# GpSimd clips every fourth probability block of the first cross-attention, with eight places for the blocks and later value products

## The chip, the cores and the metric

The kernel runs on one core of one Trainium2 chip. The metric is device time in microseconds, the median of several runs. The core's engines are TensorE (PE in the profile; PEld is its weight load), VectorE (DVE), ScalarE (ACT), GpSimd (POOL) and SyncE (SP, which here only starts transfers). Each engine works through its own list of instructions in order and waits on semaphores for the others.

## The reference

Two decoder layers on x of 2 x 512 x 256, with a context of 2 x 1024 x 192. Each layer has self-attention, cross-attention and a feed-forward part, with a layer norm behind each:

```python
x = _layernorm(x + _L0_attn_ref(x, ...))          # A0: 16 heads, causal
x = _layernorm(x + _L0_xattn_ref(x, ctx, ...))    # X0: 16 heads over 1024 keys
x = _layernorm(x + _L0_ffn_ref(x, ...))
x = _layernorm(x + _L1_attn_ref(x, ...))          # A1
x = _layernorm(x + _L1_xattn_ref(x, ctx, ...))    # X1
x = _layernorm(x + _L1_ffn_ref(x, ...))           # 8 experts, 2 chosen
```

The change is in X0:

```python
attn = jnp.einsum('bhqd,bhkd->bhqk', q, k) * scale
attn = jnp.clip(attn, -CLAMP, CLAMP)
attn = jax.nn.softmax(attn, axis=-1)
attn = jnp.where(jnp.any(jnp.isnan(attn)), 1.0 / Nkv, attn)
x = jnp.einsum('bhqk,bhkd->bqhd', attn, v).reshape(B, Nq, Cq)
return x @ Wo + bo
```

## The kernel before

A function builds one list of steps for the whole program (`build_schedule`), and each engine's block walks that list and emits the steps that are its own. So the list alone sets each engine's order. The first layer's attentions, A0 and X0, come from `paired_stream`. Their 16 heads are worked in groups of four, per batch: eight groups for A0, then eight for X0 (`PAIRS`).

X0 handles each group twice. The first pass makes scores with queries on the partitions, 16 items per group (S1, L1574, in rounded fp32), and VectorE reduces each to row maxima (M1, L1312, "halves", two rows of 512 keys at a time, negated). MN (L1318, L1319) joins and clamps them, and a TensorE transposition (unit "mt") brings them to the layout in which VectorE adds them to the queries (UD of "mt"). The second pass makes scores with keys on the partitions, 16 items per group: eight blocks j of 128 keys, each in two halves pr of two heads (S2, L1596). ScalarE takes the exponential straight into `prob_a` and sums it for the check on NaNs (E2, L1130). VectorE clips each item of 128 x 1024 to between exp(-60) and exp(60) (CL, L1326). The value product of a block takes both halves (PV, L1619) and adds into `p_out`; the last one of a group is followed by ScalarE's copy of `p_out` (DN, L1146), a transposition ("dt"), and VectorE's scaling into `normed`. While one group is in its second pass, the next is in its first.

One step n of the list holds, in this order: what empties the unit of the step before (UA, UD and the cast KF on GpSimd for the key and query operands), S2 and E2 of one item, S1 and M1 of one item of a later group, the clip of the item of the step before, at most one PV, and one unit (key, query or value product, transposition). A block's product is put into the list once its second half's clip is two steps old (`age(...) >= 2`); blocks go in order (`adds`), at most one per step. So in the steady state there is a product in every second step.

Both kinds of score block use the same ring of three places in PSUM, `p_ring` (`RING`). By the ring's order, S2 of step n waits for the maximum (M1) of step n - 2, and S1 of step n for the exponential (E2) of step n - 1 (`slot_free`). `prob_a` in SBUF has `NPT` = 6 places: E2 waits for the product of the block of six items ago. The first product of a group waits for the copy of `p_out` of the group before.

GpSimd has little to do: in A0 it clears the later keys (TM, L1042), in X0 it casts the key and query operands (KF, L1033, three per group), adds the biases (BA, L1075) and inverts deviations of the layer norms (LP, L1081, L1082). It scales a1_wq (L1050) and x1_wq (L1054) later.

The lines that matter for the order and the waits:

```python
        if adds and age("CL" if adds[0][0] == "X0" else "TM", *adds[0], 1) >= 2:
            c = adds.pop(0)
            sched.add("PV", *c)
```

```python
                    wait(act, "S2", *key)
                    if n >= NPT:
                        wait(act, "PV", *prob_list[n - NPT][:4])
```

## Time and profile before

| | |
|---|---|
| runs before | 1327.78, 1327.05, 1320.21 us; median 1327.05 |
| the profiled execution | 1310.7 us, span 1309.0 us |
| busy share of the span | TensorE 89%, VectorE 56%, ScalarE 43%, GpSimd 7% |
| mean granted clock of TensorE | 0.952 |
| X0's exponentials | 202.8 to 465.5 us of the span |
| clips of X0 on VectorE (L1326) | 128, 89.5 us, 700 ns each on average |
| maxima of X0 (L1312, 128x1024) | 128, 155.6 us, 1219 ns each |

A row of the timeline has the start in us from the span's start, the duration, the engine and line, the operation, what it writes and reads, the shapes, and in brackets how long the engine was idle before and who ended that. Times in the rows are microseconds, where ns isn't written. Instructions of one engine can overlap by about 0.1 us at their ends. The ends of matmuls are modelled, so what waits for them tells more than their durations.

### The profile page before, as it was taken

Reading aid. Unit: us, or ns where it says so; the run is one execution under the profiler, and the core shown is the slowest. Engines: PE = TensorE matmul, PEld = TensorE weight load, DVE = VectorE, ACT = ScalarE, POOL = GpSimd, SP = SyncE. Lnnn points to the kernel's source line nnn. Section 1 sums busy time; section 2 is a strip of 40 time slices with the busy share of each in tenths; the row PEclk is TensorE's granted clock in tenths of the full one; section 3 lists DMA queues with packets and bytes.
Section 4 is the critical chain, followed back from the end, with each engine's and each line's share of the span. In section 5 each row is a group of like instructions: output and inputs, shape, how many; then the busy total and the mean of one; then the engine's idle time right before and its main releaser. Section 6 shows DMA issues by size and latency. Waiting matters only on the chain.

```text
span 1309.0 us, 20311 instructions
## 1 busy us (share of the span) xinstructions
PE 1163.7 (89%) x7602; PEld 737.1 (56%) x7602; DVE 734.4 (56%) x1083; ACT 560.2 (43%) x1078; POOL 86.6 (7%) x126
## 2 busy tenths in 40 slices
PE   4998988898998864897799999999999999998886
PEld 2454443232322233786477777767777777776545
DVE  3447567888889747344265645654445554654322
ACT  1444424555555632120266654555334553453230
POOL 0112301000000002000000000000000000000120
PEclk8899778999999977999899999999999999999989
DMA  6011002000000020000533222323533333210000
GB/s 178 11 50 26 1 1 57 1 1 1 1 1 1 1 81 1 1 1 1 139 74 74 66 66 46 80 57 89 116 92 82 81 82 81 47 36 1 1 17 16
DMA packets 46819, 57.44 MB, mean 44 GB/s; under 512 B 12539, under 2 KB 25350, under 8 KB 46726
## 3 DMA queue, kind: packets, MB, share of 16 engines
q1 hardware_dynamic: 42966, 52.48, 16.4%
q10 hardware_dynamic: 3760, 3.67, 0.9%
q8 instruction: 64, 1.05, 0.3%
q14 instruction: 29, 0.24, 0.1%
HBM read 15.23 MB, written 3.15 MB: 14 GB/s over the span
## 4 chain that ended last, share of the span: by engine, by line
PE 77%; DVE 10%; issue 6%; ACT 3%; POOL 1%; DMA 1%; SPq 1%; POOLq 0%; ACTq 0%; DVEq 0%
PE p_unit L1529 20%; PE p_ring L1529 11%; PE p_ring L1630 9%; PE p_out L1653 8%; PE p_ring L1549 8%; PE p_ring L1596 7%; PE p_out L1619 6%; PE p_ring L1574 2%; PE p_unit L1715 2%; PE p_unit L1673 1%; DVE probT_b L1342 1%; PE p_ring L1588 1%; DVE stats L1245 1%; ACT prob_a L1130 1%; POOL m_z L1059 1%
## 5 line engine op out<-in xcount | busy, mean ns | idle before, releaser
L1148 ACT ACTIVATE probT_b<-p_ring 128x512 f32<-128x512 f32 x144 | 84.5, 598 | 260.0 <-PE p_ring L1630 259.6
L1312 DVE TENSOR_REDUCE halves<-p_ring 128x2 f32<-128x1024 f32 x128 | 155.6, 1219 | 44.2 <-PE p_ring L1574 44.0
L1342 DVE COPY probT_b<-p_ring 128x512 f32<-128x512 f32 x112 | 77.4, 691 | 173.7 <-PE p_ring L1630 173.7
L1294 DVE TENSOR_REDUCE nmax<-p_ring 128x2 f32<-128x1024 f32 (+1 forms) x128 | 155.9, 1218 | 23.3 <-PE p_ring L1549 23.3
L1130 ACT ACTIVATE prob_a<-p_ring 128x1024 f32<-128x1024 f32 x128 | 130.5, 1023 | 89.5 <-PE p_ring L1596 89.2
L1116 ACT ACTIVATE prob_b<-p_ring,nmax 128x512 f32<-128x512 f32 (+1 forms) x192 | 158.7, 835 | 2.9 <-DVE nmax L1294 2.6
L1549 PE MATMUL p_ring<-stacks 128*128 128x512 f32 x512 | 150.8, 416 | 4.5 <-ACT prob_b L1116 4.5
L1630 PE MATMUL p_ring<-ident,prob_b 128*128 128x128 f32 x1024 | 134.6, 274 | 0.0
L1630 PEld LDWEIGHTS p_ring<-ident,prob_b 128*128 128x128 f32 x1024 | 115.8, 141 | 27.7 <-issue 25.8
L1596 PE MATMUL p_ring<-x_q,x_kq 32*128 32x512 f32 x512 | 117.8, 646 | 0.2
L1549 PEld LDWEIGHTS p_ring<-stacks 128*128 128x128 f32 x512 | 87.0, 190 | 17.1 <-ACT prob_b L1116 5.1
L1326 DVE TENSOR_SCALAR prob_a<-prob_a 128x1024 f32<-128x1024 f32 x128 | 89.5, 700 | 8.2 <-ACT prob_a L1130 8.2
L1312 DVE TENSOR_REDUCE wide_max<-p_ring 128x2 f32<-128x256 f32 (+3 forms) x64 | 52.4, 823 | 63.7 <-PE p_ring L1567 63.7
L1574 PE MATMUL p_ring<-x_kqF 32*128 32x512 f32 x256 | 66.2, 515 | 23.4 <-ACT prob_a L1130 23.0
L1596 PEld LDWEIGHTS p_ring<-x_q,x_kq 32*128 32x128 f32 x512 | 37.5, 186 | 63.8 <-issue 45.4
L1619 PE MATMUL p_out<-prob_a,x_v 128*32 128x512 f32 x512 | 68.2, 604 | 2.7 <-issue 1.8
L1653 PE MATMUL p_out<-probT_b,a_v 128*64 128x128 f32 x1024 | 70.0, 279 | 0.0
L1653 PE MATMUL p_out<-probT_b,x_v 128*64 128x128 f32 x1024 | 69.6, 279 | 0.0
L1653 PEld LDWEIGHTS p_out<-probT_b,a_v 128*64 128x64 f32 x1024 | 54.6, 136 | 23.4 <-issue 17.5
L1653 PEld LDWEIGHTS p_out<-probT_b,x_v 128*64 128x64 f32 x1024 | 54.6, 136 | 21.9 <-issue 11.3
L1529 PE MATMUL p_unit<-ctxT,x_wk 128*128 128x512 f32 x128 | 65.2, 633 | 0.3
L1485 DVE TENSOR_TENSOR splitL_b<-p_unit,splitH_b 128x512 fp32r<-128x512 f32 x44 | 30.4, 691 | 60.8 <-ACT splitH_b L1199 54.7
(199 smaller groups left out, 1610.4 us busy)
## 6 DMA issues: line engine op xcount, KB each, us to landing
stacks<-splitH_b SPq DMA_DIRECT2D x144, 128.0 KB, 2.3
stacks<-splitL_b SPq DMA_DIRECT2D x144, 128.0 KB, 2.4
a_st<-a_image SPq DMA_DIRECT2D x64, 32.0 KB, 1.8
ctx_raw<-in_ctx ACTq DMA_DIRECT2D x1, 1536.0 KB, 15.2
x<-in_x ACTq DMA_DIRECT2D x2, 512.0 KB, 5.5
k_words<-in_L_ffn_k SPq DMA_DIRECT2D x1, 1024.0 KB, 6.7
a_wq<-in_L_attn_Wq SPq DMA_DIRECT2D x1, 1024.0 KB, 6.0
a_wo<-in_L_attn_Wpost SPq DMA_DIRECT2D x1, 1024.0 KB, 8.6
```

The source lines that it names most:

```text
L1116: ins = nc.scalar.activation(prob_b[:, n % NP_SLOTS, a * 512:a * 512 + w_all], p_scores[:, n % 2, a * 512:a * 512 + w_all], ACT.Exp, bias= ...
L1130: nc.scalar.activation(prob_place(key), slot_of("S2", key), ACT.Exp, accum_out=x0_sums[:, m:m + 1]).then_inc(done["E2"], 1)
L1294: nc.vector.tensor_reduce(nmax[:, n % 4, 0:heads], src, AX.X, ALU.max, negate=True).then_inc(done["M"], 1)
L1312: nc.vector.tensor_reduce(to, src, AX.X, ALU.max, negate=True).then_inc(done["M1"], 1)
L1342: keep_turned(dve, key, lambda o, i: nc.vector.tensor_copy(o, i)).then_inc(done["VD"], 1)
L1529: ins = nc.tensor.matmul(o, a, m, start=(n == 0), stop=(n == len(pairs) - 1))
L1549: ins = nc.tensor.matmul(p_scores[:, n % 2, 512 * a:512 * a + 512], st[:, q_at:q_at + 128], st[:, k_at:k_at + 512], start=(part == 0), sto ...
L1574: ins = nc.tensor.matmul(o[:, aa, :], x0_kqF[r:r + 32, place, 2, 128 * i:128 * i + 128], x0_kqF[r:r + 32, place, hf, :], start=True, stop= ...
L1596: ins = nc.tensor.matmul(o[:, aa, :], x0_kq[r:r + 32, place, j // 4, 128 * (j % 4):128 * (j % 4) + 128], x0_q2[r:r + 32, G % 2, :], start= ...
L1619: ins = nc.tensor.matmul(p_out[32 * a:32 * a + 32, lo:T], v, prob_place((*key, a // 2))[:, a % 2, at:at + T - lo], start=(c == 0), stop=end)
L1630: ins = nc.tensor.transpose(p_turn[:, half, 128 * j:128 * j + 128], prob_b[:, n % NP_SLOTS, 128 * bl:128 * bl + 128], ident[:, :])
L1653: ins = nc.tensor.matmul(p_out[rows * a:rows * a + rows, 128 * i:128 * i + 128], values(L, b, h, j), probT[:, n % places, 4 * in_tile + j ...
```

## The change

GpSimd gets a new kind of step, CP, for the second half (pr = 1) of every odd block j of X0: four of each group's 16 items, 32 of 128. It runs the same `tensor_scalar` (max, then min) on the same place of `prob_a`. The product of such a block is put into the list once its clip is four steps old instead of two; since blocks go in order, the even block behind it is late too. `prob_a` has eight places instead of six. The new function `clipped_by` says whose clip a product waits for.

```diff
--- before.py
+++ after.py
@@ -52,7 +52,7 @@
 NP_SLOTS = 3
 RING = 3
 HELD = 3
-NPT = 6
+NPT = 8
 UNDER = 60.0
 LOW, HIGH = float(np.exp(-UNDER)), float(np.exp(UNDER))
 NC1 = 7
@@ -110,6 +110,11 @@
 def prob_items(grp):
 
     return [(*grp, j, pr) for j in range(NKV // 128 if grp[0] == "X0" else 3) for pr in range(2)]
+
+
+def clipped_by(it):
+
+    return "TM" if it[0] == "A0" else "CP" if it[3] % 2 == 1 and it[4] == 1 else "CL"
 
 
 def blocks_at(j):
@@ -193,7 +198,7 @@
                     sched.add("MN", *it[:3])
                 owed.insert(0, ("mt", *it[:3]))
         for it in clean:
-            sched.add("CL" if it[0] == "X0" else "TM", *it)
+            sched.add(clipped_by(it), *it)
             if it[4] == 1:
                 adds.append(it[:4])
         clean = fresh
@@ -203,7 +208,7 @@
             owed.append(("dt", *grp))
             if grp[2] % 2:
                 owed.append(("rb", *grp[:2], grp[2] // 2))
-        if adds and age("CL" if adds[0][0] == "X0" else "TM", *adds[0], 1) >= 2:
+        if adds and age(clipped_by((*adds[0], 1)), *adds[0], 1) >= (4 if clipped_by((*adds[0], 1)) == "CP" else 2):
             c = adds.pop(0)
             sched.add("PV", *c)
             if c[3] == prob_items(c[:3])[-1][3]:
@@ -693,7 +698,7 @@
             "UA": "unit_emptied_by_act", "UD": "unit_emptied_by_dve", 
             "BA": "bias_added", "LS": "variances_ready", "LP": "deviations_inverted",
             "LN": "x_normalised", "XA": "x_rounded", "XD": "x_rest_ready", "FW": "signs_ready",
-            "FS": "hidden_split", "CL": "probs_clipped", "DN": "outputs_kept", "NF": "nans_counted", "GN": "nans_replaced",
+            "FS": "hidden_split", "CL": "probs_clipped", "CP": "probs_clipped_by_pool", "DN": "outputs_kept", "NF": "nans_counted", "GN": "nans_replaced",
             "ZD": "gates_by_dve", "ZA": "gates_by_act", "ZP": "roots_ready",
         }
         done = {k: sem(v) for k, v in names.items()}
@@ -1031,6 +1036,10 @@
                     if 4 * b + g >= HELD:
                         wait(pool, "S1", *max_items(PAIRS[8 + 4 * b + g - HELD])[-1])
                     nc.gpsimd.tensor_copy(x0_kqF[:, place, part, :], x0_kq[:, place, part, :]).then_inc(done["KF"], 1)
+                elif kind == "CP":
+                    wait(pool, "E2", *key)
+                    t = prob_place(key)
+                    nc.gpsimd.tensor_scalar(t, t, LOW, HIGH, ALU.max, ALU.min).then_inc(done["CP"], 1)
                 elif kind == "TM":
                     j = key[3]
                     wait(pool, "E2", *key)
@@ -1602,7 +1611,7 @@
                     L, b, g, j = key
                     grp = key[:3]
                     for pr in range(2):
-                        wait(pe, "CL" if L == "X0" else "TM", *key, pr)
+                        wait(pe, clipped_by((*key, pr)), *key, pr)
                     if j == 0:
                         back = pair_back(grp, 1)
                         if back:
```

The list changes TensorE's order. Here is TensorE's list in a stretch of X0 from one query product ("xT,x_wq") to the copy's transposition ("ident,raw") and the first products of the next group. `x_q,x_kq` is S2, `x_kqF` S1, `prob_a,x_v` the value product. Before:

```order
L1529 MATMUL p_unit<-xT,x_wq 128x512 x2
L1596 MATMUL p_ring<-x_q,x_kq 128x512 x2
L1574 MATMUL p_ring<-x_kqF 128x512 x2
L1619 MATMUL p_out<-prob_a,x_v 32x512 x4
L1596 MATMUL p_ring<-x_q,x_kq 128x512 x2
L1574 MATMUL p_ring<-x_kqF 128x512 x2
L1596 MATMUL p_ring<-x_q,x_kq 128x512 x2
L1574 MATMUL p_ring<-x_kqF 128x512 x2
L1619 MATMUL p_out<-prob_a,x_v 32x512 x4
L1685 MATMUL p_unit<-ident,raw 128x128 x4
```

The same stretch of the change, from the same query product (its lines are numbered nine higher):

```order
L1538 MATMUL p_unit<-xT,x_wq 128x512 x2
L1605 MATMUL p_ring<-x_q,x_kq 128x512 x2
L1583 MATMUL p_ring<-x_kqF 128x512 x2
L1605 MATMUL p_ring<-x_q,x_kq 128x512 x2
L1583 MATMUL p_ring<-x_kqF 128x512 x2
L1605 MATMUL p_ring<-x_q,x_kq 128x512 x2
L1583 MATMUL p_ring<-x_kqF 128x512 x2
L1628 MATMUL p_out<-prob_a,x_v 32x512 x4
L1605 MATMUL p_ring<-x_q,x_kq 128x512 x2
L1583 MATMUL p_ring<-x_kqF 128x512 x2
L1628 MATMUL p_out<-prob_a,x_v 32x512 x4
```

Before, the last product of a group (the first of the two above) and the first product of the next stand two steps apart, with the copy of `p_out` in the step between; now they stand in neighbouring steps, and everywhere in X0 the products stand in pairs, with two steps without one behind them.

VectorE's list in the same stage, before (`TENSOR_SCALAR prob_a` is the clip, `TENSOR_REDUCE` the maximum):

```order
L1312 TENSOR_REDUCE halves<-p_ring 128x2
L1326 TENSOR_SCALAR prob_a<-prob_a 128x1024
L1312 TENSOR_REDUCE halves<-p_ring 128x2
L1326 TENSOR_SCALAR prob_a<-prob_a 128x1024
L1312 TENSOR_REDUCE halves<-p_ring 128x2
L1326 TENSOR_SCALAR prob_a<-prob_a 128x1024
L1312 TENSOR_REDUCE halves<-p_ring 128x2
L1326 TENSOR_SCALAR prob_a<-prob_a 128x1024
```

And of the change:

```order
L1335 TENSOR_SCALAR prob_a<-prob_a 128x1024
L1321 TENSOR_REDUCE halves<-p_ring 128x2
L1335 TENSOR_SCALAR prob_a<-prob_a 128x1024
L1321 TENSOR_REDUCE halves<-p_ring 128x2
L1335 TENSOR_SCALAR prob_a<-prob_a 128x1024
L1321 TENSOR_REDUCE halves<-p_ring 128x2 x2
L1335 TENSOR_SCALAR prob_a<-prob_a 128x1024
```

One clip in four is gone, so two maxima follow each other there; the clip stands on GpSimd, between its casts:

```order
L1042 TENSOR_SCALAR prob_a<-prob_a 128x1024 x3
L1038 CAST x_kqF<-x_kq 128x512
L1042 TENSOR_SCALAR prob_a<-prob_a 128x1024
L1038 CAST x_kqF<-x_kq 128x512 x2
L1042 TENSOR_SCALAR prob_a<-prob_a 128x1024 x3
```

GpSimd's list had only the casts between the bias addition and the layer norm behind X0.

## Rows read from the trace of the kernel before

**Rows 1.** Busy time of each engine in two head groups of X0 (columns: span, busy times with counts, clock, DMA).
```profile
275.27:310.63 35.36, 32.28 (x188) 10.90 (x190) 29.99 (x37) 20.26 (x37) 1.85 (x4) 1.00 0.00 1
...
414.91:445.61 30.70, 27.31 (x176) 8.72 (x178) 27.51 (x36) 18.16 (x34) 0.00 (x0) 1.00 0.00 1
```

**Rows 2.** The chain that ended last from 245 to 387 us, its shares by line.
```profile
by line: PE p_ring L1596 33.8%; PE p_out L1619 22.7%; PE p_unit L1529 16.8%; issue 12.6%; PE p_ring L1574 7.0%; ACT prob_a L1130 2.9%; PE p_unit L1685 1.7%; PE p_unit L1693 1.7%; PE p_unit L1715 0.8%; ACTq L719 0.3%
```

**Rows 3.** Waits in the group 275.27 to 310.63 us (total us, times, longest us).
```profile
ACT prob_a L1130 <- PE p_ring L1596: 11.7, 11, 2.0
PEld p_ring L1574 <- ACT prob_a L1130: 7.1, 6, 1.6
...
DVE halves L1312 <- PE p_ring L1574: 5.3, 8, 2.1
```

**Rows 4.** Timeline of ScalarE in the clean stretch (start, duration, line, operation).
```profile
296.35 1.02 ACT L1130 ACTIVATE prob_a<-p_ring 128x1024 f32<-128x1024 f32 x1 [1.64 <-PE p_ring L1596]
297.27 0.20 ACT L1130 ACTIVATION_READ_ACCUMULATOR prob_a<-p_ring 128x1 f32 x1
...
300.12 1.02 ACT L1130 ACTIVATE prob_a<-p_ring 128x1024 f32<-128x1024 f32 x1 [1.65 <-PE p_ring L1596]
```

**Rows 5.** Timeline of TensorE's matmuls, same stretch.
```profile
297.52 0.50 PE L1574 MATMUL p_ring<-x_kqF 32*128 32x512 f32 x2 [0.75 <-ACT prob_a L1130]
297.95 1.06 PE L1619 MATMUL p_out<-prob_a,x_v 128*32 128x512 f32 x8
298.95 0.70 PE L1596 MATMUL p_ring<-x_q,x_kq 32*128 32x512 f32 x2
...
299.41 1.13 PE L1596 MATMUL p_ring<-x_q,x_kq 32*128 32x512 f32 x6
```

**Rows 6.** Timeline of VectorE, same stretch.
```profile
297.54 0.68 DVE L1326 TENSOR_SCALAR prob_a<-prob_a 128x1024 f32<-128x1024 f32 x1
298.14 1.22 DVE L1312 TENSOR_REDUCE halves<-p_ring 128x2 f32<-128x1024 f32 x1
299.27 0.68 DVE L1326 TENSOR_SCALAR prob_a<-prob_a 128x1024 f32<-128x1024 f32 x1
300.17 1.22 DVE L1312 TENSOR_REDUCE halves<-p_ring 128x2 f32<-128x1024 f32 x1 [0.21 <-PE p_ring L1574]
```

**Rows 7.** Groups of GpSimd's instructions by shape (busy us, mean ns of one).
```profile
L1042 POOL TENSOR_SCALAR_AFFINE_SELECT prob_a<-prob_a 128x256 f32<-128x256 f32 x32 | 13.0, 410 | 50.3 <-ACT prob_a L1134 50.3
...
L1042 POOL TENSOR_SCALAR_AFFINE_SELECT prob_a<-prob_a 128x512 f32<-128x512 f32 x16 | 10.2, 641 | 24.2 <-ACT prob_a L1134 24.2
...
L1050 POOL TENSOR_SCALAR a_wq<-a_wq 128x2048 f32<-128x2048 f32 x1 | 5.5, 5464 | 6.9 <-DMA a_wo<-in_L_attn_Wpost 6.9
...
L1054 POOL TENSOR_SCALAR x_wq<-x_wq 128x1024 f32<-128x1024 f32 x1 | 2.8, 2795 | 34.8 <-DMA x_bo<-in_L_xattn_bout 34.8
```

**Rows 8.** Timeline of GpSimd, the bias addition of the second batch.
```profile
212.36 2.34 POOL L1075 TENSOR_TENSOR x<-x,x_bo 128x1024 f32<-128x1024 f32 x1 [11.36 <-PE p_unit L1673]
```

**Rows 9.** Timeline of VectorE beside it: the clip.
```profile
212.46 2.79 DVE L1326 TENSOR_SCALAR prob_a<-prob_a 128x1024 f32<-128x1024 f32 x1
```

**Rows 10.** Timeline of all engines, the bias addition of the first batch.
```profile
137.04 2.36 POOL L1075 TENSOR_TENSOR x<-x,x_bo 128x1024 f32<-128x1024 f32 x1
...
138.05 1.23 DVE L1312 TENSOR_REDUCE wide_max<-p_ring 128x2 f32<-128x1024 f32 x1 [0.71 <-PE p_ring L1567]
```

**Rows 11.** ScalarE's copy of p_out, by its line (ns: min/median/max).
```profile
L1146 ACT ACTIVATE raw<-p_out x16: 590/592/603, 77.2 to 479.0; 128x512 f32<-128x512 f32 x16
```

**Rows 12.** End of X0: ScalarE's last sum, then VectorE's NaN count and replacement.
```profile
465.34 0.19 ACT L1130 ACTIVATION_READ_ACCUMULATOR prob_a<-p_ring 128x1 f32 x1
...
465.56 0.29 DVE L1330 TENSOR_TENSOR x_sums<-x_sums 128x128 f32<-128x128 f32 x1 [0.37 <-ACT prob_a L1130]
...
467.39 1.29 DVE L1338 COPY_PREDICATED outT_n<-x_nan,x_mean 128x1024 f32<-128x1024 int32 x1
```

**Rows 13.** The chain in order of time: a key product.
```profile
307.61 1.91 PE p_unit L1529 x4
```

## The prediction

> **What bounds the kernel now.** I first took the stage: the change touches the clips of X0, the first cross-attention, and the step at which its value products are issued. By the groups of rows for one head group, a group of sixteen steps lasts 35.36 us, TensorE has work for 32.28, VectorE for 29.99 and ScalarE for 20.26, at the full clock of 1.00 (2.4 GHz) [rows 1]. There are seven such intervals between the eight head groups, most of this length; the last, where the maxima run out, has 30.70 us [rows 1]. The chain of this stage is made of TensorE's products, 12.6% of issue and 2.9% of exponentials; no VectorE line is among the names of this stretch [rows 2]. The waits name the loop: ScalarE waits 11.7 us per group for score blocks (L1596), and TensorE waits for ScalarE's exponential to empty a place of the ring (7.1 us), while VectorE waits 5.3 us for maximum blocks [rows 3].
>
> The timeline shows the loop, which takes two steps. An exponential starts at 296.35, its sum is read by 297.47, the maximum block that takes its place in the ring starts at 297.52 [rows 4, 5]. The value product starts at 297.95 (0.43 later) and the next score block at 298.95 (1.00 later). The next exponential starts at 300.12, 1.17 later [rows 5, 4]. Sum: 1.12 + 0.05 + 0.43 + 1.00 + 1.17 = 3.77 us for two steps, 7.53 for four. VectorE is not in this loop but runs close beside it: a maximum occupies it 1.13 us (298.14 to 299.27), a clip 0.60 (297.54 to 298.14), so four of each need 6.92 of 7.53 us; its one idle gap per two steps is 0.21 us [rows 6]. The second maximum ends at 299.36, and a score block follows at once at 299.41 [rows 6, 5]. So VectorE has about 0.6 us to spare in four steps, and what delays it by more delays everything.
>
> **The change, part by part.**
>
> *32 of 128 clips leave VectorE.* VectorE saves 0.60 us of its order for each: 2.4 us per group, 0.6 in each four steps. By itself that is worth nothing, since the loop above has no clip in it.
>
> *GpSimd clips instead.* The trace has no such clip. The nearest row is the scaling of x1_wq, the same shape with one operation instead of two: 2.80 us; double the width took 5.46, so it is linear [rows 7]. From below, the triangle clearing of 256 and 512 elements took 0.41 and 0.64 us, which makes 1.10 us for 1024; from above I take 5.46, as if each operation were a pass of its own. I take 2.80, since that row is the same instruction. GpSimd's own time is covered: the loop of four steps is 7.5 us, its only other work here are three short casts per group, and the value product now waits four steps behind the clip. With 5.46 us it is covered only just.
>
> *What GpSimd's clip does to VectorE.* This is the term that decides. One row of the trace has a VectorE clip beside a long GpSimd operation: the bias addition ran from 212.36 to 214.70, and the clip that started at 212.46 took 2.79 us instead of 0.68: it ended 0.55 us behind GpSimd's end [rows 8, 9]. It did not run slower, it stood still. A maximum beside the same addition (137.04 to 139.40) took its usual 1.23 us [rows 10]. So I take it that a clip on VectorE waits until GpSimd's instruction has ended, and a maximum does not. The Trainium skill (SBUF — State Buffer, "Who interferes with whom") says this too: a tensor_scalar in a two-port mode and a GpSimd instruction exclude each other for the whole instruction, and a tensor_reduce never contends; the trace agrees, 2.79 us against 0.68.
>
> Between two maxima VectorE nearly always has a clip due. If GpSimd's clip starts as a maximum starts, 1.13 us of it lie under the maximum and the next clip waits 2.80 - 1.13 = 1.67 us. If it starts right in front of a VectorE clip, that one waits 2.80. The exponential of such a block ends at 297.47 and VectorE's next clip starts at 297.54 [rows 4, 6], so at first it is the long case; once VectorE lags, it is the short one. Four steps then cost VectorE 4 x 1.13 + 3 x 0.60 + 1.67 to 2.80 = 8.0 to 9.1 us, against 7.53: VectorE becomes the bound, and late maxima hold the ring's places, so that score blocks and exponentials are late next. Over a group: four waits of 2.25 (the middle) are 9.0 us, minus 2.4 saved, is 6.6 us more in VectorE's order. Its idle time there is 5.3 us [rows 3]; much of it lies behind the three key and query products, where it can be used only if a wait falls there. I estimate that half to two thirds are used, 3.3 us. That leaves +3.3 us per group, and +23 us over seven intervals. Bounds: with all 5.3 used and short waits 4 x 1.67 - 2.4 - 5.3 = -1.0, no loss; with none used and long waits 11.2 - 2.4 = +8.8 per group, +62.
>
> *Value products later and in pairs.* An odd block's product now waits four steps, and the even one behind it in the list follows a step later. The order rows show pairs in neighbouring steps, then two steps without one. Two things follow. In the clean stretch the loop gets shorter where VectorE allows it: with the same pieces, the two exponentials beside the value products are hidden and the walk of four steps comes to 6.85 us instead of 7.53. Against that, the first value product of a head group now stands one step behind the last of the group before, and both use p_out: it must wait for ScalarE to copy p_out (DN). ScalarE does that behind the exponential of the step between. TensorE then waits from the score block on for 1.17 + 1.02 + 0.59 = 2.8 us instead of 0.98 [rows 4, 5, 11], +1.8 us once per group. Before, a whole step without a product lay between. Two of the dearer steps (a value product and a key or query product of 1.91 us [rows 13]) now stand side by side as well, which I estimate at +0.6 per group; the net without any blocking (two clean stretches of four steps per group) is 8 x 1.8 + 7 x 0.6 - 14 x 0.68 = +9 us. With VectorE as the bound neither the gain nor most of the loss shows, since both waits run at the same time. I take 0 here; the bounds are -10 and +15.
>
> *Eight places instead of six.* An exponential waits for the product of eight blocks ago. TensorE's order puts that product at least two steps ahead, so there is no wait, as there was none before. Without the two places the later products would stop ScalarE.
>
> *The end of the stage.* The last clip is GpSimd's. The last exponential's sum is read at 465.53, and GpSimd runs from 465.6 to 468.4. VectorE's NaN count starts at the same time, and reads twice from SBUF [rows 12]. If it is blocked as well, replacing the NaNs (467.39) and the projection behind it come up to 2.8 us later; if not, the last value product comes about 1 us later. I take +2.
>
> Sum: 23 + 0 + 2 = +25 us. The profiled execution took 1310.7 us (span 1309.0), so its counterpart is 1336. The three timed runs lie higher, 1320.2 to 1327.8 with a median of 1327.05, so the predicted median is 1352.
>
> **The rivals.**
>
> *GpSimd's two-operation clip is much longer than 2.80.* For it: the row that I use has one operation, and GpSimd is slow at that shape already. At 3.5 us each wait is 0.7 longer, 28 x 0.7 = +20: 1372. At 5.46 four steps cost 6.32 + 4.33 = 10.65 us instead of 7.53, 28 x 3.1 = +87: about 1414. Against it: the rows for 1024 and 2048 show a rate set per element, which a second operation on the same element need not change.
>
> *The clip is short or doesn't block.* Then only the order counts, +9: 1336, no measurable change. For it: GpSimd's clearing of the same tile runs at a pace of 1.10 us per 1024, and such a clip would hide under one maximum. Against it: 2.80 for the nearest instruction, and rows 8 and 9. The Trainium skill (GPSIMD Engine Reference, "Engine selection") calls GpSimd about as fast as the line for one input; by that rule the clip would take about 1 us and the time be this rival's. The 2.80 us row speaks against it.
>
> *Faster.* If the blocking is absent or falls mostly into the product stretches, and the pairs save their 0.68 us in every four steps, 28 x 0.68 = -19: 1308. It decides once 20 of the 28 cycles gain and the wait for the p_out copy hides behind the ring's own wait. Against it: that copy stands behind an exponential in ScalarE's order, every time.
>
> **How the numbers follow.** Blocking at about 2.80 us (median 1352, own range 1335 to 1365): 0.60. A longer clip: 0.20. Short or unblocked: 0.14. Faster: 0.06. The range 1334 to 1386 takes in the first case, longer clips up to about 4 us, and the upper half of the third; it leaves out the rest, some 0.2. One per cent is 13 us, about what a measurement of this kernel can tell from no change. Slower by more than that (over 1340): 0.53 + 0.20 + 0.02 = 0.75. Faster (under 1314): 0.06. Within: 0.19.
>
> **What would show it.** Right: GpSimd rows of the clip near 2.8 us, 32 of them; VectorE clips in the same stage with a median of 0.68 but some thirty of 2 us or more, each ending about 0.55 us behind a GpSimd clip; VectorE's waits for maximum blocks down from 5.3 to 2 us or less per group; a group of about 38.5 instead of 35.36 us; VectorE clips and maxima in the chain of this stage. The step on the products is right if TensorE waits at the first value product of each group for ScalarE's copy of p_out. Wrong: VectorE clips that stay at 0.68 beside GpSimd's, or GpSimd clips of 4 us and more. Stages before 200 us and behind 470 us should differ by no more than the shift.

## The result, and the profile after

The changed kernel took 1351.18 us in the median of four runs (1340.28 to 1373.43). The kernel before took 1323.63 us in four (1319.42 to 1327.78), and the ratio is 1.0214, with an interval of 1.0161 to 1.0266: slower by 2.1%. A median here is of all executions of a kernel, while a ratio with its interval leaves out those over 1.5% above the kernel's fastest (one of four here, and one of 1944.64 us in pool_two below), so it is not the quotient of the medians. The forecast time of 1352 is met. The mechanism that I gave most of it to is not what happened.

The page of the profiled execution after, first the span, the busy times and the granted clock of TensorE in 40 slices, then from the groups VectorE's maxima (L1321), GpSimd's clips (L1042) and VectorE's clips (L1335):

```profile
span 1351.5 us, 20309 instructions
...
PE 1196.3 (89%) x7602; PEld 749.6 (55%) x7602; DVE 718.0 (53%) x1051; ACT 561.0 (42%) x1078; POOL 202.9 (15%) x158
...
PEclk8995866879999986799899999999999999999998
...
L1321 DVE TENSOR_REDUCE halves<-p_ring 128x2 f32<-128x1024 f32 x128 | 155.0, 1219 | 75.8 <-PE p_ring L1583 74.6
...
L1042 POOL TENSOR_SCALAR prob_a<-prob_a 128x1024 f32<-128x1024 f32 x32 | 117.1, 3658 | 107.5 <-ACT prob_a L1139 107.5
...
L1335 DVE TENSOR_SCALAR prob_a<-prob_a 128x1024 f32<-128x1024 f32 x96 | 72.0, 750 | 14.3 <-ACT prob_a L1139 14.3
```

A GpSimd clip is longer than I took it for (3.66 us in the mean, forecast 2.80). VectorE's clips are hardly longer than before: 750 ns in the mean, 683 in the median. TensorE has the same 7602 matmuls, yet 1196.3 us of busy time, where the kernel before had 1163.7. Its mean granted clock was 0.923, before 0.952.

The head groups of X0, each from its first exponential of the second pass to the next group's (the columns as in [rows 1]):

```profile
218.67:259.89 41.22, 34.59 (x164) 12.81 (x168) 31.07 (x37) 19.10 (x36) 14.15 (x5) 0.71 0.08 21
259.89:302.22 42.33, 36.70 (x184) 11.41 (x185) 28.05 (x33) 19.75 (x36) 16.77 (x8) 0.84 0.00 1
302.22:341.38 39.16, 33.41 (x188) 11.05 (x190) 28.15 (x33) 20.46 (x37) 16.23 (x8) 0.96 0.00 1
341.38:377.95 36.57, 31.52 (x184) 10.46 (x186) 27.97 (x33) 19.76 (x36) 16.23 (x8) 1.00 0.00 1
377.95:415.54 37.59, 31.84 (x188) 10.83 (x190) 28.15 (x33) 20.47 (x38) 16.24 (x8) 1.00 0.00 1
```

Before, the same seven intervals lasted 37.1, 35.4, 35.4, 35.4, 35.4, 33.6 and 30.7 us, all but the first at the clock of 1.00 ([rows 1] has the third and the seventh). The first one before:

```profile
202.79:239.90 37.11, 31.51 (x172) 11.29 (x176) 32.16 (x40) 19.12 (x35) 2.74 (x2) 0.91 0.05 10
```

After, the seven sum to 262.5 us against 242.8. Three of them ran at a lower clock and carry 14.9 of the 19.7 us; the four at 1.00 are longer by 1.2, 2.2, 0.9 and 0.5. The last part, up to the last exponential, has 25.0 us against 18.8. So X0 is 26 us longer, and what lies behind it is not (845 us in both). The 15.9 us by which X0 starts later in this execution lie ahead of every clip and product that the change moves; only the eight places reach that far back, since A0 uses them too. In a second execution of the same kernel (below) they are 2.3. In order_only, with the same order and places, X0 starts 3.9 us earlier than before, and in places, with the eight places alone, 17.1 later. This part varies from trace to trace by more than its own size, and I don't count it to the change.

The waits of the group 377.95 to 415.54 (total us, times, longest), to be held against [rows 3], and the chain from 341.4 to 481 us, against [rows 2]:

```profile
ACT prob_a L1139 <- PE p_ring L1605: 12.0, 14, 2.4
...
DVE halves L1321 <- PE p_ring L1583: 9.2, 6, 2.7
...
PE p_out L1628 <- issue: 1.9, 1, 1.9
```

```profile
by line: PE p_ring L1605 27.5%; PE p_out L1628 18.0%; issue 12.6%; DVE halves L1321 11.1%; PE p_unit L1538 11.0%; PE p_ring L1583 6.4%; DVE prob_a L1335 5.1%; DVE wide_max L1328 2.0%; PE p_unit L1702 1.8%; ACT prob_a L1139 1.4%; PE p_unit L
```

I had forecast that VectorE's wait for maximum blocks falls from 5.3 to 2 us or less. It rose to 9.2: over a group VectorE has more time to spare than before. It is on the path in places, though: its maxima and clips, which weren't among the names of [rows 2], are 16% of the chain now. New among the waits is their last line: a wait of TensorE's at a value product, once in the group. Here it stands, TensorE first, then ScalarE (start, duration, ..., idle time before it in brackets):

```profile
389.49 0.70 PE L1605 MATMUL p_ring<-x_q,x_kq 32*128 32x512 f32 x2
389.63 0.50 PE L1583 MATMUL p_ring<-x_kqF 32*128 32x512 f32 x2
390.02 0.59 PE L1605 MATMUL p_ring<-x_q,x_kq 32*128 32x512 f32 x2
392.47 1.07 PE L1628 MATMUL p_out<-prob_a,x_v 128*32 128x512 f32 x8 [1.85 <-issue]
```

```profile
390.66 1.02 ACT L1139 ACTIVATE prob_a<-p_ring 128x1024 f32<-128x1024 f32 x1 [1.09 <-PE p_ring L1605]
391.58 0.19 ACT L1139 ACTIVATION_READ_ACCUMULATOR prob_a<-p_ring 128x1 f32 x1
391.68 0.59 ACT L1155 ACTIVATE raw<-p_out 128x512 f32<-128x512 f32 x1
```

The group's first value product starts at 392.47, 0.2 us behind the end of ScalarE's copy of `p_out`, which stands behind an exponential; TensorE did nothing for 1.85 us. The profile names "issue" as the releaser, which says only that it shows no event for it; the copy's end is what fits. This line's group, summed over the program, has 13.0 us of such idle time, seven times 1.85. Before it had 1.8, a single wait of the same kind at the first product of the last group (450.80). After, then before:

```profile
L1628 PE MATMUL p_out<-prob_a,x_v 128*32 128x512 f32 x512 | 74.5, 656 | 13.1 <-issue 13.0
```

```profile
L1619 PE MATMUL p_out<-prob_a,x_v 128*32 128x512 f32 x512 | 68.2, 604 | 2.7 <-issue 1.8
```

So six of the seven are new, 11.2 us. That is the wait that I priced right, +1.8 us per group, and then counted as 0.

### The profile page after: what moved, and what is told of

Read it like the earlier page. It is cut to its first block, busy times and chain, and to the rows that moved or that the text cites. A ratio compares the mean times of both kernels' runs of the same rounds, so it can differ in the third digit from the quotient of the medians.

```text
span 1351.5 us, 20309 instructions
## 1 busy us (share of the span) xinstructions
PE 1196.3 (89%) x7602; PEld 749.6 (55%) x7602; DVE 718.0 (53%) x1051; ACT 561.0 (42%) x1078; POOL 202.9 (15%) x158
## 4 chain that ended last, share of the span: by engine, by line
PE 77%; DVE 11%; issue 6%; ACT 3%; DMA 1%; POOL 1%; SPq 1%; POOLq 0%; DVEq 0%; ACTq 0%
PE p_unit L1538 20%; PE p_ring L1538 11%; PE p_ring L1639 9%; PE p_out L1662 8%; PE p_ring L1558 8%; PE p_ring L1605 6%; PE p_out L1628 6%; DVE halves L1321 2%; PE p_ring L1583 2%; PE p_unit L1724 2%; PE p_unit L1682 1%; PE p_ring L1597 1%; DVE prob_a L1335 1%; DVE probT_b L1351 1%; PE p_ring L1576 1%
## 5 line engine op out<-in xcount | busy, mean ns | idle before, releaser
L1321 DVE TENSOR_REDUCE halves<-p_ring 128x2 f32<-128x1024 f32 x128 | 155.0, 1219 | 75.8 <-PE p_ring L1583 74.6
L1042 POOL TENSOR_SCALAR prob_a<-prob_a 128x1024 f32<-128x1024 f32 x32 | 117.1, 3658 | 107.5 <-ACT prob_a L1139 107.5
L1605 PE MATMUL p_ring<-x_q,x_kq 32*128 32x512 f32 x512 | 130.2, 684 | 0.0
L1090 POOL TENSOR_SCALAR veps<-mv 128x4 f32<-128x4 f32 x12 | 3.4, 281 | 722.1 <-DVE mv L1376 722.1
L1321 DVE TENSOR_REDUCE wide_max<-p_ring 128x2 f32<-128x256 f32 (+3 forms) x64 | 52.6, 824 | 75.5 <-PE p_ring L1576 75.4
L1583 PE MATMUL p_ring<-x_kqF 32*128 32x512 f32 x256 | 69.3, 546 | 19.3 <-ACT prob_a L1139 19.0
L1628 PE MATMUL p_out<-prob_a,x_v 128*32 128x512 f32 x512 | 74.5, 656 | 13.1 <-issue 13.0
L1335 DVE TENSOR_SCALAR prob_a<-prob_a 128x1024 f32<-128x1024 f32 x96 | 72.0, 750 | 14.3 <-ACT prob_a L1139 14.3
L1605 PEld LDWEIGHTS p_ring<-x_q,x_kq 32*128 32x128 f32 x512 | 40.9, 200 | 60.7 <-issue 27.1
L1662 PEld LDWEIGHTS p_out<-probT_b,x_v 128*64 128x64 f32 x1024 | 54.6, 136 | 21.9 <-issue 11.3
```

What stands on the lines that cost most here:

```text
L1042: nc.gpsimd.tensor_scalar(t, t, LOW, HIGH, ALU.max, ALU.min).then_inc(done["CP"], 1)
L1321: nc.vector.tensor_reduce(to, src, AX.X, ALU.max, negate=True).then_inc(done["M1"], 1)
L1583: ins = nc.tensor.matmul(o[:, aa, :], x0_kqF[r:r + 32, place, 2, 128 * i:128 * i + 128], x0_kqF[r:r + 32, place, hf, :], start=True, stop= ...
L1605: ins = nc.tensor.matmul(o[:, aa, :], x0_kq[r:r + 32, place, j // 4, 128 * (j % 4):128 * (j % 4) + 128], x0_q2[r:r + 32, G % 2, :], start= ...
L1628: ins = nc.tensor.matmul(p_out[32 * a:32 * a + 32, lo:T], v, prob_place((*key, a // 2))[:, a % 2, at:at + T - lo], start=(c == 0), stop=end)
L1662: ins = nc.tensor.matmul(p_out[rows * a:rows * a + rows, 128 * i:128 * i + 128], values(L, b, h, j), probT[:, n % places, 4 * in_tile + j ...
```

## The experiments

Two theories stood against each other. *Blocking*: GpSimd's clip holds VectorE's up. *Order*: the new places of the value products, above all of the first of a group behind the copy of `p_out`, cost the time, whoever clips.

### after_again: the changed kernel once more

> The changed kernel once more, to see how much of its profiled +42.6 us (1353.3 against 1310.7) is the granted clock. In its trace only four of eight head groups ran at the full clock of 1.00, and those are 0.5 to 2.2 us longer than before, +4.8 us together; the other four at clocks of 0.71 to 0.96 are 4 to 7 us longer, and the part ahead of the first second-pass item was 15.9 us longer at a lower clock too. If the clock is chance, the ratio of this kernel to the one before comes to 1.01 or less and the group times at full clock repeat. If a lower clock comes with the change, the ratio stays near 1.02 and the mean clock under 0.94.

1357.23 us against 1316.76, ratio 1.0255 (1.0177 to 1.0334). X0 lasts 288.9 us (287.6 in the first profile), with the intervals 42.4, 42.3, 37.6, 36.6, 39.2, 34.5, 31.2 and the clocks 0.72, 0.84, 1.00, 1.00, 0.96, 1.00, 1.00. The loss and its shape repeat; which group has the lower clock changes.

### order_only: the changed order, all clips on VectorE

```diff
-                elif kind == "CL":
+                elif kind in ("CL", "CP"):
...
-                    nc.vector.tensor_scalar(pr, pr, LOW, HIGH, ALU.max, ALU.min).then_inc(done["CL"], 1)
+                    nc.vector.tensor_scalar(pr, pr, LOW, HIGH, ALU.max, ALU.min).then_inc(done[kind], 1)
```

> The changed order of value products and the eight places, but all 128 clips on VectorE (in the changed kernel's order). If GpSimd's clip is what costs (by blocking VectorE's), this kernel is near the kernel before: a group at full clock at most 36 us, total within +9 us. If the order of the products costs, a full-clock group takes 36.6 and 37.6 us in turn as in the changed kernel, and the total is the changed kernel's within 0.5%, or a little more since VectorE has its four clips back.

1368.49 us, ratio 1.0299 (1.0228 to 1.037). With no clip on GpSimd the whole loss is there, so blocking is not needed for it. Its fifth interval, and of TensorE's timeline one first product of a group:

```profile
363.02:407.03 44.01, 39.84 (x188) 12.11 (x189) 30.00 (x37) 20.40 (x37) 1.84 (x4) 0.81 0.00 1
```

```profile
294.58 1.06 PE L1624 MATMUL p_out<-prob_a,x_v 128*32 128x512 f32 x8 [1.85 <-issue]
```

The same 1.85 us, and no group at the full clock. Behind the first interval, the recorded stretches at the lower level (1.2 GHz) begin at 255.2, 296.1, 337.1, 378.0, 422.4, 456.5 and 487.3 us, and the seven standstills end at 254.2, 294.6, 335.5, 377.5, 421.6, 456.5 and 486.1: each of them has such a stretch behind it, by at most 1.6 us.

### even: GpSimd's clips, but every product of X0 four steps late

With one delay for all blocks, a product stands in every second step again, and two steps lie between the groups, as before the change.

```diff
-        if adds and age(clipped_by((*adds[0], 1)), *adds[0], 1) >= (4 if clipped_by((*adds[0], 1)) == "CP" else 2):
+        if adds and age(clipped_by((*adds[0], 1)), *adds[0], 1) >= (4 if adds[0][0] == "X0" else 2):
```

> GpSimd keeps its 32 clips, but every block's product waits four steps behind its clip, so that products stand in every second step again, as before the change. If the pairs and the neighbouring first product cost the time, a full-clock group is back at 35.4 us and the total is within 0.5% of the kernel before. If GpSimd's clip costs by itself, the group stays at 36.5 us or more and the total at +10 us or more.

1328.41 us, ratio 1.0071 (1.004 to 1.0102): over two thirds of the loss are gone with all 32 clips still on GpSimd. Its windows:

```profile
207.70:249.15 41.45, 34.85 (x164) 12.42 (x168) 31.22 (x37) 19.12 (x36) 14.68 (x5) 0.71 0.08 21
249.15:284.50 35.35, 31.55 (x184) 10.27 (x185) 28.43 (x33) 19.66 (x36) 17.84 (x8) 1.00 0.00 1
```

From the second interval on a group takes 35.4 us, as before. What is left in X0 is the first interval (41.5 against 37.1 us, clock 0.71 against 0.91) and 1.1 us in the last part. No wait for the copy stands in that first interval, in any kernel here, so the 4.1 us that the changed kernel loses there aren't the copy's either.

### even_vector: the same order, all clips on VectorE

The edits of order_only and even together.

> The control of the run named even: same order, all clips on VectorE. Both theories expect the kernel before, 35.4 us per group and 1.000 +- 0.005 in the ratio. What even has over it is the price of GpSimd's clips; what it has over the kernel before is the price of products two steps later and of eight places.

1329.47 us, ratio 1.0088 (1.0058 to 1.0117). Its intervals are 41.5, 35.4, 35.4, 35.4, 35.4, 33.6 and 30.7 us. I had expected 1.000 +- 0.005, and it is slower than that; like even it has the longer first interval. With and without GpSimd's clips the kernel is the same within what the intervals tell apart. The 32 clips taken from VectorE are worth nothing that these runs can show, and done on GpSimd they cost nothing that they can show, when the order is held.

### gap: the changed kernel, with a step between the copy and the next product

```diff
+        late = 4 if adds and clipped_by((*adds[0], 1)) == "CP" else 2
+        copied = not adds or adds[0][0] == "A0" or adds[0][3] or age("DN", *PAIRS[order[adds[0][:3]] - 1]) >= 1
-        if adds and age(clipped_by((*adds[0], 1)), *adds[0], 1) >= (4 if clipped_by((*adds[0], 1)) == "CP" else 2):
+        if adds and copied and age(clipped_by((*adds[0], 1)), *adds[0], 1) >= late:
```

> The changed kernel, but the first value product of a head group goes into the list only a step behind the one with ScalarE's copy of p_out, as before the change; pairs stay elsewhere. In the changed kernel TensorE stands still for 1.85 us in front of that product in every group. Order theory, wait for the copy as its main part: a full-clock group falls from 36.6 and 37.6 us to 35.5 or less, and the total to within 0.5% of the kernel before, since the clock holds. Order theory, pairs as the main part: the group stays above 36 us and the total above +1%. If the lower clock is a thing of GpSimd's clips, the clock stays under 0.94 and the total near +2%.

1323.28 us against 1318.98, ratio 1.0008 (0.9966 to 1.005). One edit, which moves only the first product of each group (and what it pushes), takes the loss away, to within the half per cent of the interval. Windows, and the group of the value product:

```profile
205.35:247.66 42.31, 34.89 (x164) 12.46 (x168) 30.89 (x37) 19.11 (x36) 13.62 (x5) 0.72 0.08 21
247.66:283.17 35.51, 31.23 (x184) 10.29 (x185) 28.10 (x33) 19.64 (x36) 16.77 (x8) 1.00 0.00 1
...
423.25:452.40 29.15, 27.09 (x176) 9.22 (x176) 26.26 (x32) 18.25 (x35) 14.64 (x4) 1.00 0.00 1
452.40:474.88 22.48, 19.69 (x120) 5.39 (x118) 8.22 (x13) 16.13 (x34) 14.48 (x4) 0.92 0.00 1
```

```profile
L1630 PE MATMUL p_out<-prob_a,x_v 128*32 128x512 f32 x512 | 71.8, 634 | 2.7 <-issue 1.6 <-DVE prob_a L1337 0.2 <-ACT raw L1157 0.2
```

The idle time at the value products is 2.7 us again, and the intervals are at 1.00 from the second to the seventh. The pairs stay in this kernel, so they tell what pairs are worth by themselves: 35.5 us against 35.4, about nothing. In its trace X0 as a whole is still 7.9 us longer than before: 5.2 in the first interval (42.3 us), 3.7 in the last part (22.5 against 18.8), and 1.0 less between them.

### gap_vector: gap, all clips on VectorE

> The run named gap with all clips back on VectorE: what GpSimd's 32 clips are worth in the paired order. In gap's order the pairs shorten the ring's loop and VectorE has 6.9 us of work in each four steps, so its clips can now bind. If GpSimd's relief counts, this kernel is 3 to 8 us slower than gap (0.3 to 0.6%), with a full-clock group above 35.5 us; if it doesn't, the same.

1326.58 us against 1318.21, ratio 1.0054 (1.0022 to 1.0087), groups of 35.2 to 35.5 us at 1.00, where I had expected more than 35.5 if GpSimd's relief counts. Gap had 1.0008 with an interval that overlaps this one. If GpSimd's clips bring anything, it is some 0.4%, and these runs don't settle it.

### neighbour: the kernel before, with only its last product of a group moved

This puts the last product of a group in the step beside the first of the next and changes nothing else of note: no GpSimd clip, no pairs, the first product where it was.

```diff
-NPT = 6
+NPT = 8
...
-        if adds and age("CL" if adds[0][0] == "X0" else "TM", *adds[0], 1) >= 2:
+        late = 3 if adds and adds[0][0] == "X0" and adds[0][3] == 7 else 2
+        if adds and age("CL" if adds[0][0] == "X0" else "TM", *adds[0], 1) >= late:
```

> The kernel before with eight places and one edit: the last value product of each head group is put one step later, into the step just ahead of the next group's first product. No pairs elsewhere, all clips on VectorE. It isolates the wait for the copy of p_out. If that wait is the cause: 1.85 us of standstill at each of seven boundaries, 13 us at full clock, a group near 37 us, and more where the clock falls too, ratio 1.01 to 1.025. If the loss of the changed kernel was rather the pairs, or the products crowded into the key and query steps: within 0.5% of the kernel before.

1347.37 us, ratio 1.0211 (1.0155 to 1.0268): the size of the whole change out of one step of one product per group, with no clip on GpSimd. Its third and fourth interval, then TensorE around one standstill:

```profile
280.56:317.65 37.09, 32.02 (x188) 10.47 (x189) 29.98 (x37) 20.35 (x38) 1.84 (x4) 1.00 0.00 1
317.65:355.79 38.14, 34.02 (x184) 10.37 (x185) 29.80 (x37) 19.84 (x36) 1.84 (x4) 0.96 0.00 1
```

```profile
330.16 1.91 PE L1620 MATMUL p_out<-prob_a,x_v 128*32 128x512 f32 x8 [1.85 <-issue]
332.00 1.22 PE L1597 MATMUL p_ring<-x_q,x_kq 32*128 32x512 f32 x2
...
335.58 1.06 PE L1620 MATMUL p_out<-prob_a,x_v 128*32 128x512 f32 x8
```

Here both parts of the cost can be read apart. A group at the full clock is 37.1 us, 1.75 more than 35.36: that is the standstill itself. In the group from 317.65 the product right behind the standstill took 1.91 us, the next one 1.06: the granted clock fell to the 1.2 GHz level at 330.3 and was back by then, and the group is 38.1. The sixth and the seventh interval ran at 0.95 and 0.90, the second at 0.88. Against the trace of places, from which this kernel differs by that one step alone, X0 is 27.9 us longer: 2.2 in the first interval, 11.3 as more standstill, and the rest, 14.4, under the lower clock and in the last part.

### places: the kernel before, with eight places

```diff
-NPT = 6
+NPT = 8
```

> The kernel before with eight places for probabilities instead of six, nothing else. All theories expect no change: ratio 1.000 +- 0.004, 35.4 us per group. If it is slower by 0.7 to 0.9% like the runs with evenly late products, those owe their rest to the places (or to the later products' addresses) and not to the two steps.

1318.79 us against 1318.98, ratio 1.0022 (0.9994 to 1.0051); groups of 35.35 us. The places alone change nothing that the interval shows, as the prediction had it, and neighbour's loss is not theirs.

### pool_two: GpSimd's clips, every product two steps late

```diff
+        if adds and age(clipped_by((*adds[0], 1)), *adds[0], 1) >= 2:
```

> GpSimd's 32 clips with the order of before: products two steps behind every clip, so GpSimd's clip of 3.62 us must end within 3.77 us of two steps. If GpSimd's clips are free and the order is the whole cost, 1.000 +- 0.005 and 35.4 us per group, at most 36 where the product now waits for GpSimd (visible as a wait of TensorE's value product for L1042's line). If it takes 2% more, GpSimd's clips cost after all.

1336.96 us, ratio 1.0136 (1.0093 to 1.0178). That is neither the 1.000 nor the 2% that I had set against each other: it is what GpSimd's clip costs when its cover is taken away. The middle groups take 35.62 us, only 0.26 more than before; the first takes 41.5, as in even, and the last part, where nothing but clips and products is left, 28.2 against 18.8. The waits there, and the clips' durations (ns: min/median/max):

```profile
PE p_out L1628 <- POOL prob_a L1042: 8.4, 4, 2.7
```

```profile
L1042 POOL TENSOR_SCALAR prob_a<-prob_a x32: 3622/4149/4154, 231.1 to 496.6; 128x1024 f32<-128x1024 f32 x32
```

The two extra steps that the change gives such a block are needed, but for the last part of the stage rather than the middle.

### tt_beside: the kernel before, with a tensor_tensor of GpSimd's beside the same clips

In place of its clip GpSimd does an addition on a tile of its own, on the same signal; the clips all stay on VectorE.

```diff
+                elif kind == "CL" and key[3] % 2 == 1 and key[4] == 1:
+                    wait(pool, "E2", *key)
+                    link(nc.gpsimd.tensor_tensor(beside[:, :], beside[:, :], beside[:, :], ALU.add))
```

> The kernel before, all clips on VectorE, and GpSimd adds a spare tile of 128x1024 to itself beside 32 of them (tensor_tensor, work that nobody reads), at the place where the change puts its clips. The blocking rule of the prediction, from the one row with a tensor_tensor: VectorE clips that start inside take up to 2.8 us, and the total goes up by 20 us or more. If blocking is only an effect of where that one clip fell, or is short as it is beside GpSimd's tensor_scalar (0.87 instead of 0.68 us), the total stays within 5 us.

1325.66 us, ratio 1.0057 (1.0021 to 1.0094). The middle groups have 35.6 and 36.0 us. One collision, GpSimd then VectorE:

```profile
253.78 2.42 POOL L1038 TENSOR_TENSOR beside<-beside 128x1024 f32<-128x1024 f32 x1 [2.95 <-ACT prob_a L1135]
```

```profile
254.37 1.22 DVE L1317 TENSOR_REDUCE halves<-p_ring 128x2 f32<-128x1024 f32 x1
255.50 1.25 DVE L1331 TENSOR_SCALAR prob_a<-prob_a 128x1024 f32<-128x1024 f32 x1
```

The clip ends at 256.75, 0.55 us behind GpSimd's end, as in [rows 8, 9]: the rule that I took from there holds for this kind of instruction where GpSimd's starts first. But the collision costs 0.57 us, not 1.67, since most of GpSimd's time is already gone under a clip that started with it and a maximum. Of the 32 additions 24 had a clip start inside, which took 1.16 to 1.99 us, and the second to the sixth interval lost 0.3 to 0.65 us each. Real blocking, all through the stage, is worth about half a per cent, more than the 5 us of one expectation and far from the 20 of the other.

### tuned: a delay for each block by hand, with gap's rule

The delays are 5, 3, 5, 4, 4, 4, 5, 2 for the eight blocks of a group.

> The changed kernel's clips with a table of delays per block (5, 3, 5, 4, 4, 4, 5, 2 steps) and the copy's gap of gap: pairs where no key or query product stands, single products beside those. Walked with the pieces of the trace (1.17, 1.12, 0.43, 1.00, and 1.91 for a key product) it saves 1.0 to 1.5 us per group at full clock, 4 to 8 us in all: ratio to the kernel before 0.994 to 0.997, a group near 34.5 us. If the clock of the first groups falls as in gap, no gain is left.

1322.9 us against 1318.21, ratio 1.0041 (1.0008 to 1.0075), where I had expected 0.994 to 0.997. Windows of the second interval and the last part:

```profile
245.05:279.71 34.66, 31.98 (x184) 10.69 (x185) 28.19 (x33) 19.91 (x36) 16.25 (x8) 1.00 0.00 1
...
447.77:476.88 29.11, 27.29 (x120) 6.38 (x120) 8.82 (x13) 16.43 (x33) 14.49 (x4) 0.71 0.00 1
```

The second to the fifth interval alternate between 34.7 and 35.3 us, so the loop can be made a little shorter than before (3.0 us over the six intervals behind the first). The last part gives it all back and more: 29.1 us against 18.8, at a clock of 0.71. No kernel here is faster than the one before.

### one_op: even, with one operation in GpSimd's clip

It leaves out the minimum of GpSimd's clips.

```diff
-                    nc.gpsimd.tensor_scalar(t, t, LOW, HIGH, ALU.max, ALU.min).then_inc(done["CP"], 1)
+                    nc.gpsimd.tensor_scalar(t, t, LOW, None, ALU.max).then_inc(done["CP"], 1)
```

> The run named even, but GpSimd's clips do the maximum alone and leave the minimum out. If the second operation is what made its clip 3.62 us instead of the 2.80 of the scaling with one operation, the clip is 2.8 us here. VectorE clips beside it take 0.87 us or less.

One execution, 1328.09 us, as even. The group of the clip:

```profile
L1042 POOL TENSOR_SCALAR prob_a<-prob_a 128x1024 f32<-128x1024 f32 x32 | 99.6, 3111 | 106.2 <-ACT prob_a L1139 106.2
```

The mean is 3.11 us, and an undisturbed one has 2.76 to 2.78, the 2.80 of [rows 7]. So the second operation adds 0.85 us (3.62 against 2.77): neither nothing, as I took it, nor a second pass. The rest of the mean comes from 20 clips of 3.3 us and more that started 0.01 us behind one of VectorE's (last section). VectorE's own clips beside it took up to 1.29 us, more than the 0.87 expected.

## Why the prediction was right and wrong

**The bound.** Right for the kernel before: TensorE, the ring and ScalarE form the loop. (The maximum that ends at 299.36 is the first of [rows 6], not the second.) VectorE now has 28 us of work in a group instead of 30, and the full-clock groups of even and gap against those of their controls, 35.2 to 35.6 us in all four, show that this is worth nothing. The paired order, however, brings VectorE's maxima and clips into the chain, 16% of it after, as one of my signs had said, and not because GpSimd blocks them: gap_vector, without any clip on GpSimd, has them there too (24% from 254 to 429 us).

**GpSimd's clip costs 2.80 us.** Wrong by 0.8: 3.62. The upper bound of 5.46 held. It didn't matter, since with four steps' delay nobody waited for it; this is the line's own view after, with an empty list of waiters behind it:

```profile
L1042 POOL TENSOR_SCALAR prob_a<-prob_a x32: 3620/3622/4151, 231.4 to 507.4; 128x1024 f32<-128x1024 f32 x32
...
who waited for it (us, times):
```

So the rival of a longer clip also fails: at 3.5 us it asked for 1372, and the clip was that long, but the price wasn't paid.

**A VectorE clip waits until GpSimd's instruction ends, 1.67 to 2.80 us, +3.3 per group, +23.** This step failed. I carried one row, of a tensor_tensor [rows 8, 9], to a tensor_scalar. Three VectorE clips of the changed kernel, and then the three GpSimd clips in which they start:

```profile
388.81 0.87 DVE L1335 TENSOR_SCALAR prob_a<-prob_a 128x1024 f32<-128x1024 f32 x1
...
476.71 1.14 DVE L1335 TENSOR_SCALAR prob_a<-prob_a 128x1024 f32<-128x1024 f32 x1
...
483.37 0.69 DVE L1335 TENSOR_SCALAR prob_a<-prob_a 128x1024 f32<-128x1024 f32 x1 [0.31 <-ACT prob_a L1139]
```

```profile
388.09 3.62 POOL L1042 TENSOR_SCALAR prob_a<-prob_a 128x1024 f32<-128x1024 f32 x1 [1.91 <-ACT prob_a L1139]
...
473.67 3.62 POOL L1042 TENSOR_SCALAR prob_a<-prob_a 128x1024 f32<-128x1024 f32 x1 [4.22 <-ACT prob_a L1139]
481.41 3.62 POOL L1042 TENSOR_SCALAR prob_a<-prob_a 128x1024 f32<-128x1024 f32 x1 [4.11 <-ACT prob_a L1139]
```

The clip that starts 0.72 us into GpSimd's takes 0.87 and ends 2.04 us ahead of GpSimd's end. The one that starts 1.96 in is not delayed at all (0.69). The one that starts 3.04 in takes 1.14 and ends 0.56 behind GpSimd's end. A collision therefore costs 0, 0.2 or 0.5 us in this trace (up to 0.8 in other kernels, as in tuned, 1.49 us for a clip that starts 0.09 in). The Trainium skill (SBUF — State Buffer, "Who interferes with whom") says that whoever comes first keeps the other out for its whole instruction; for GpSimd's tensor_tensor the runs agree (tt_beside), for its tensor_scalar they don't, and the measurement decides. In place of +3.3 us per group, even against even_vector shows at most 0.14. All 96 VectorE clips together took 72.0 us, 6.4 more than 96 of 683 ns; 2.1 of that is the one beside the bias addition, which was there before. The waits themselves were over-sized too: where GpSimd's instruction does block to its end (tt_beside), the clips that start inside were delayed by 0.5 to 1.3 us, not by 1.67 to 2.80, and the total rose by half a per cent.

**The wait for the copy of `p_out`, +1.8 us per group.** The size was right: 1.85 measured, at the place named, "at the first value product of each group". Wrong was what I did with it. I took 0 "with VectorE as the bound", since both waits would run at the same time; with VectorE not the bound it counts in full, 1.75 us in neighbour's groups. My sum also counted eight such waits; seven stand in the changed kernel, and one of them was there before. And I left out what hangs on them: behind a standstill TensorE ran at the 1.2 GHz level for a while in some groups. At the full clock the whole change is +1.2, +2.2, +0.9 and +0.5 us per group, some 8 us if seven groups are taken at their mean of 1.2, near the +9 of my unblocked sum. The lower clock and the tail made 26 of it. That is why "the clip is short or doesn't block", the rival that was right on the mechanism, was wrong on its time of 1336.

**Pairs save 0.68 per four steps, crowding costs 0.6 per group.** Taken together they were forecast at -0.8 per group (0.6 - 2 x 0.68); with the gap restored, a group with pairs has 35.5 us against 35.36. What fits is that the walk of 6.85 us left no room for VectorE, whose lines stand in gap's chain, but no run tests that. The rival "faster" had its second condition met in gap (the copy hidden), and still gained nothing.

**Eight places cost nothing.** Right (places).

**The tail, +2.** Too small: the last part of X0 took 6.2 us more. What I had looked at, the NaN count and replacement beside GpSimd's last clip, was hardly hindered. GpSimd's last clip and VectorE's replacement in the middle of it:

```profile
507.42 3.72 POOL L1042 TENSOR_SCALAR prob_a<-prob_a 128x1024 f32<-128x1024 f32 x1 [1.34 <-ACT prob_a L1139]
```

```profile
508.92 1.31 DVE L1347 COPY_PREDICATED outT_n<-x_nan,x_mean 128x1024 f32<-128x1024 int32 x1
```

The replacement took 1.31 us, against 1.29 in [rows 12]. What grew is the stretch ahead of it: one 1.85 us standstill up to 489.1, where before one of 1.84 stood too, and then half speed from 490.7 for 6.8 us. Gap, where the clock of this part was 0.92, has 3.7 us more there than before, so some of it belongs to the later products and not to the copy.

**The sum.** 23 + 0 + 2 came to +25, the runs show +27.5 in the medians and the first trace +26 in X0. By causes it should have read: 0 for blocking, about +8 for the order at full clock, and the rest, some 18, for the granted clock in X0 and the last part. Of that rest 4.1 us are the first interval's, which even and gap have without the standstills; neighbour shows that the standstills with what follows them are enough for a loss of this size. The time was met by luck: a term of 23 that wasn't there stood in for one that I had set to 0 and one that I had left out. A right total from a wrong largest term is worth little for the next kernel; two of the signs that I had named (VectorE's waits, clips of 2 us) came out the other way, and they are what a reader should check ahead of the total.

**What is not settled.** Why the first interval runs at 0.71 to 0.72 in after, even, gap and their controls but at 0.91 before and 0.82 in places: its product starts later there (164 matmuls in it instead of 172), but neighbour, with 172, had 0.75. All kernels, the one before too, have one standstill of 3.35 us there, for VectorE's layer norm (before, up to 208.1), and a fall of the clock beside it; what differs is how long the clock stays down, 6.8 us before, 13.7 in places, 20.5 in neighbour and 23.9 in after and even. Why order_only, with the clips on VectorE, had a lower clock in more groups than after. And which standstills bring the clock down: in the traces of after, after_again, order_only and neighbour, 18 of 28 were followed within 1.6 us by the lower level or fell together with it, the others of the same length (after, 392.47) were not.

## To carry to other kernels

When a step moves in a hand-written order, look at what else uses its buffer. A first product that must wait for the copy-out of its accumulator needs a step without a product between, and one such wait in each 35 us of X0 cost 2% of the whole kernel here. Price a wait of TensorE's above its own length, since what follows may run at half clock (neighbour: 11.3 us more standstill than places, and 25.7 us lost behind the first interval); and don't set a wait to 0 because another one is expected to cover it, unless that other one is sure. A rule read from one row belongs to that row's instruction: ask for the same pair of operations before it is multiplied by 28.

## What the runs showed of the hardware

A standstill of 1.85 us in an otherwise busy stretch can be followed by the 1.2 GHz level: in neighbour the product behind it took 1.91 us instead of 1.06. In after, after_again, order_only and neighbour the level fell at 18 of 28 such standstills. With the standstills gone (gap, even and their controls), the intervals from the second to the seventh all ran at 1.00.

GpSimd's two-operation tensor_scalar keeps VectorE's out in two pieces, not as a whole. Over all kernels with such clips, VectorE clips that started up to 0.9 us into one of 3.62 ended 1.58 us behind its start, those that started 0.95 to 2.1 in took their usual 0.69, and those from 2.7 in ended 0.55 behind its end. With one operation (one_op, 2.76 us) the same two pieces lie closer together: a clip that started 0.96 in took 0.69, one that started 2.02 in took 1.29 and ended 0.55 behind GpSimd's end. It also works the other way: where VectorE's clip had just begun, GpSimd's took 4.15 us instead of 3.62, as in even, GpSimd then VectorE:

```profile
259.34 4.15 POOL L1042 TENSOR_SCALAR prob_a<-prob_a 128x1024 f32<-128x1024 f32 x1 [2.95 <-ACT prob_a L1139]
```

```profile
259.32 0.68 DVE L1335 TENSOR_SCALAR prob_a<-prob_a 128x1024 f32<-128x1024 f32 x1
...
263.09 0.95 DVE L1335 TENSOR_SCALAR prob_a<-prob_a 128x1024 f32<-128x1024 f32 x1
```

For GpSimd a clip of 128 x 1024 costs 3.62 us where VectorE needs 0.68, five times as much, and 2.77 with one operation. Why the two kinds of GpSimd instruction differ in what they keep out was not tried.
